# Running counts in PSUM beside an indirect scatter: one edit to a graph-network kernel's setup

## What is computed

```
edge_index = stack([src, dst])
h = relu(layernorm(x));  x = x + L0(h)   # messages x[dst] * filter(edge_weight), summed over src
h = relu(layernorm(x));  x = x + L1(h)   # two attention layers, softmax over the edges of one dst
h = relu(layernorm(x));  x = x + L2(h)   # edge MLP with edge_attr_64, mean over dst
h = relu(layernorm(x));  x = x + L3(h)   # 8-head attention over the edges of one dst
```

## Time and profile before

| | before |
|---|---|
| median of 3 runs | 7402.07 us |
| the profiled execution | 7404.54 us, span 7402.5 us |
| DVE busy over the span | 3299.0 us (45%) |
| POOL busy over the span | 5000.4 us (68%) |
| setup: next stage's first instruction | at 1304 us |
| L440, POOL's scatter | 782 DMAs, 791.2 us busy, 1012 ns each |
| L647, DVE's scans | 439 and 427 ns each |

### The profile page before, as it was taken

How to read it: one execution, slowest core, us unless ns; L and a number is a source line. 1 busy time by engine, 2 the same in 40 slices (tenths; PEclk the granted TensorE clock), 3 DMA queues, 4 the chain that set the end, 5 groups by cost and what they waited for, 6 DMA issues and landing times. The chain is left out here.

```text
span 7402.5 us, 89274 instructions
## 1 busy us (share of the span) xinstructions
PE 3331.8 (45%) x17325; PEld 2957.3 (40%) x17326; DVE 3299.0 (45%) x10231; ACT 1691.6 (23%) x4176; POOL 5000.4 (68%) x5176
## 2 busy tenths in 40 slices
PE   2200000444443864444434444445777775444443
PEld 1100000444443753444434444434777664344443
DVE  8777732333323663333344333335333336544445
ACT  2200000211111963222223222223222224000000
POOL 1677777677777726777755777764777770777775
PEclk9655555666666986555556555566666677666666
DMA  6122234444443624444434444433444440444443
GB/s 225 57 92 91 96 97 151 153 156 156 155 154 133 218 79 136 129 134 131 133 91 129 133 133 130 133 100 107 134 135 134 134 128 30 132 132 133 132 132 105
DMA packets 507505, 942.53 MB, mean 127 GB/s; under 512 B 204347, under 2 KB 240683, under 8 KB 507304
## 3 DMA queue, kind: packets, MB, share of 16 engines
q1 hardware_dynamic: 349288, 637.41, 25.9%
q0 software_dynamic: 158144, 304.31, 15.8%
HBM read 673.90 MB, written 270.84 MB: 128 GB/s over the span
## 5 line engine op out<-in xcount | busy, mean ns | idle before, releaser
L1371 POOL DMA_INDIRECT edge_buf<-node_table,ixr x1664 | 1571.6, 944 | 619.4 <-issue 507.9
L1371 POOL DMA_INDIRECT Y<-node_table,ixr x1664 | 1569.7, 943 | 521.1 <-issue 519.9
L1111 DVE TENSOR_TENSOR ACC<-ACC,bank 128x129 f32 (+2 forms) x3744 | 1092.9, 292 | 1102.2 <-PE bank L1098 469.2
L1279 POOL DMA_INDIRECT layer_messages<-edge_buf,ixr x832 | 809.3, 973 | 295.7 <-issue 263.0
L1538 PE MATMUL bank<-adc,turned_buf 128*128 x2496 | 340.3, 195 | 1476.1 <-issue 571.7
L440 POOL DMA_INDIRECT edge_records<-edge_buf x782 | 791.2, 1012 | 255.1 <-issue 246.2
L1538 PEld LDWEIGHTS bank<-adc,turned_buf 128*128 128x128 bf16 x2496 | 257.0, 103 | 1606.7 <-issue 1552.4
L1098 PE MATMUL bank<-edge_buf,Y 128*128 128x129 f32 (+2 forms) x3744 | 821.1, 406 | 142.7 <-ACT edge_buf L1524 96.5
L1098 PE MATMUL bank<-Y 128*128 128x129 f32 (+1 forms) x3328 | 763.1, 420 | 158.6 <-ACT Y L1524 88.7
L1098 PEld LDWEIGHTS bank<-edge_buf,Y 128*128 128x128 f32 x3744 | 764.0, 309 | 173.1 <-DVE ACC L1111 136.7
L1098 PEld LDWEIGHTS bank<-Y 128*128 128x128 f32 x3328 | 713.4, 323 | 181.5 <-issue 89.0
(11 more groups left out here) (279 smaller groups left out, 5319.1 us busy)
## 6 DMA issues: line engine op xcount, KB each, us to landing
Y<-onehots SPq DMA_DIRECT2D x416, 512.0 KB, 3.6
turned_buf<-onehots_turned SPq DMA_DIRECT2D x312, 256.0 KB, 3.8
edge_buf<-edge_records SPq DMA_DIRECT2D x208, 288.0 KB, 2.9
onehots<-Y SPq DMA_DIRECT2D x104, 512.0 KB, 2.7
layer_messages<-ACC SPq DMA_DIRECT2D x28, 1584.0 KB
XI<-layer_messages SPq DMA_DIRECT2D x78, 528.0 KB, 3.7
edge_records<-H SPq DMA_DIRECT2D x1, 29952.0 KB
onehots_turned<-turned_buf SPq DMA_DIRECT2D x104, 256.0 KB
```

Of the source, the lines that this page charges most:

```text
L1111: nc.vector.tensor_tensor(acc, acc, places.at(q, j, w), ALU.add).then_inc(added, 1)
L1279: pool.indirect_dma_start(msg_d, bass.IndirectOffsetOnAxis(ap=ixr[h][:, j:j + 1], axis=0), rows[h][:, j, 0:MW], None, bounds_check=SLOTS - ...
L1371: pool.indirect_dma_start(ring[q][:, j, 0:w], None, table, bass.IndirectOffsetOnAxis(ap=ixr[q][:, j:j + 1], axis=0)).then_inc(rows_in[q], 16)
```

## The change

For chunks 1 to 6 the tile `cum` of each h moves from SBUF to PSUM (bank 2 for h = 0, bank 3 for h = 1, 2 x 112 fp32 columns each). The second tensor of the scan, which the bypass does not use, becomes 112 columns of bank 1, set to zero once ahead of the loop. `eq`, `offs` and `slots` stay in SBUF. Chunk 0 stays as it was.

```diff
+            cums_psum = [bank[2 + h][:, 0:2 * CH].rearrange("p (q c) -> p q c", q=2) for h in range(2)]
+            unread = bank[1][:, 0:CH]
...
+                            running = cums if helped else cums_psum
+
                             def step(n, work):
                                 for h in range(2):
-                                    work(h, eqs[h], cums[h], bass.ds(i * 2 + h, 1))
+                                    work(h, eqs[h], running[h], bass.ds(i * 2 + h, 1))
...
                             def running_count(h, eq, cum, b):
                                 for q in range(2):
-                                    v.tensor_tensor_scan(cum[:, q, :], eq[:, q, :], eq[:, q, :], offs[0:EP, q, b],
-                                                         ALU.add, ALU.bypass).then_inc(count, 1)
+                                    v.tensor_tensor_scan(cum[:, q, :], eq[:, q, :], eq[:, q, :] if helped else unread,
+                                                         offs[0:EP, q, b], ALU.add, ALU.bypass).then_inc(count, 1)
...
                         slot_rows(0, st.then)
 
+                        st.then(v.memset(unread, 0.0))
                         with dve.Fori(1, CHUNKS) as c:
```

## The result

The kernel with the change takes 7372.8 us (median of seven runs, 7369.9 to 7375.9), the kernel before in the same comparison 7401.5 us (7399.5 to 7413.7). The ratio is 0.996, 95% interval 0.9949 to 0.9971: faster by 28.7 us. The first four experiments ran on a chip on which the kernel before takes 8976.4 us, the others on two chips on which it takes 7402.0 and 7401.1 us.

The account below looks back on a forecast made before the run. POOL's indirect DMAs were taken to bound the setup. The profiled 7404.5 us less 28.1 of delay is 7376.4; with the median of the runs 2.5 us under it, the forecast was 7374 us, range 7366 to 7392.

Parts of the forecast that it names:

- The path: Setup: POOL's 782 indirect DMAs set its pace from 250.5 us on; SyncE's padding ends last but moves with them.
- The term: POOL's scatter, L440: the whole delay of DMAs starting under scan, mask or addition goes, 28.1 us.
- The cause of the delay: L440's DMAs starting under L647, L655 or L658, with two SBUF tensor inputs, wait for the instruction's rest: 1.064 against 0.972 us.
- the prediction's own exception: One scatter DMA of 3.98 us at 1197.4 us starts under the relu L211; its 3.0 us stay, as the diff leaves L211 alone.
- the scans' case: Rival, chunks 1 to 6: scans, also reading `offs` from SBUF, go on delaying; 16.6 of 28.1 us stay, 7391 us; 5%.
- DVE at no price: DVE's rounds, chunks 1 to 6: ten instructions a round read or write PSUM at no added time.
- The cover: DVE's rounds beside the scatter: each may grow by 0.70 us before POOL waits; today's end is met again at 0.87 us.
- The formula: If DVE sets the pace at T a chunk, the last scatter starts at 250.5 + 6T and ends 144.9 us later.
- The parts: Shares of the 28.1 us by DMA starts in chunks 1 to 6: scans 16.6, masks 5.7.
- Mask: Rival, chunks 1 to 6: masks, whose SBUF tensor is the second input, go on delaying; 5.7 of 28.1 us stay, 7380 us; 5%.
- No effect: Rival, POOL's scatter: the delay comes from DVE's being busy with fp32 streams as such and stays whole; 7402 us; 5%.
- DVE as the bound: Rival, DVE's rounds: PSUM doubles the scan's streaming part, 1.27 us a round; the last DMA ends 59 us late, 7461 us; 6%.

Follow-up runs that it names:

- The first four experiments: Changed kernel with only the scan's second tensor, or only the counts, in PSUM; or with two more additions a round (one or two SBUF inputs): 8987.7, 8988.9, 9026.9, 9031.7 us.
- e7: Changed kernel with SyncE's last two padding writes issued behind its first load instead of its last: 7372.1 us, ratio 0.9958 to the kernel before.
- e5: Changed kernel with four more additions a round in chunks 1 to 6, each with one SBUF input: 7407.0 us, ratio 1.0005 to the kernel before.
- The scans alone: Changed kernel with the counts back in SBUF, only the scan's unused second tensor in PSUM: 7384.3 us, ratio 0.9977 to the kernel before.
- the rest alone: Changed kernel with the counts in PSUM but each scan reading `eq` twice, without the memset: 7384.9 us, ratio 0.9977 to the kernel before.
- e1: Changed kernel with the counts back in SBUF, only the scan's unused second tensor in PSUM: 8987.7 us against 8976.4, ratio 1.0011.

## Why the prediction was right

*The path.* POOL's pace was said to set the setup's end, with the padding moving along. The end of the scatter's last DMA went from 1288.2 to 1260.7 us, the padding's issue came 27.5 us earlier and the next stage too, at 1276.56 (forecast: DMA near 1260, stage near 1276). That SP's padding ends last was read rightly too; e7 shows 4.4 us for it.

*The term.* 28.1 us were forecast, the busy time fell by 791.2 - 763.5 = 27.7 us. That all of it would go rested on rows of later stages, in both orders of the operands; both orders hold in L659 and L662. One of those rows shows less than was read from it: the DMA at 3001.07 us starts 8 ns before the instruction of L1111 that it was put under. The trace as a whole bears the reading out, with 85 DMAs of L1371 that start under L1111 with over 0.2 us left and take 0.944 us (median), at most 0.947. The median moved by 28.7 us, 1 us more than the setup, which the runs' own spread covers.

*The cause of the delay.* Two SBUF tensors were named as what the three lines have in common. For these lines that was right, and the change needed no more. As a rule for all of DVE it was too narrow: the prediction's own exception, the relu L211, has one SBUF tensor, and `equal_to` (L643) delays as well. The argument from L643 against the scans' case (it has a tensor and a pointer in SBUF and its starts take 0.97) therefore proved nothing, since nearly all its starts came too late in it to be delayed. The conclusion held all the same: scans with one SBUF tensor and the pointer `offs` delay none of 172 starts. "The start waits for the rest" was right but for the last 0.13 to 0.20 us.

*DVE at no price.* Scans 439 to 442 ns, masks 393 to 400, additions 392 to 387: right to within 7 ns an instruction. The column update became cheaper (182 to 155 ns) and the two comparisons L647 too (619 to 599 ns together), for which the prediction had nothing; a round starts every 4.79 us instead of 4.88. Behind the cover it is worth nothing. The Trainium skill (page "VectorE: DVE Perf Modes", section "The TRN2 errata") has fixed costs of 58 cycles from SBUF and 120 from PSUM at 0.96 GHz, which is, as an estimate, 65 ns more an instruction. The additions of 128x224 show a difference of -5 ns, and here the measurement decides.

*The cover.* "It decides from 0.87 us a round": e5 added 0.86 to the round of the kernel before (5.74 against 4.88) and came out at 1.0005. The formula was 6 us short there, for the reason given above.

*The parts.* Here the prediction was wrong, and the forecast did not need them, because everything went. It shared the 28.1 us out as 16.6 for the scans and 11.5 for the rest. The scans alone gave 16.1 (791.2 - 775.1), the rest alone 18.4. What failed is the assumption that the places of POOL's starts in DVE's round stay as they are when a part of the delay goes.

*The rivals.* Mask and scans: both refuted by the table above. No effect and DVE as the bound: refuted on the chips of 7401 us. On the first chip DVE set the pace in the traces that were taken there, but through idle time at issue, not through the price of PSUM, which was the mechanism I had named; the change itself did not run there.

## What to carry to other kernels

Where GpSimd's indirect DMAs set the pace, look at each one's duration against what runs on VectorE at its start: if the longer ones begin under two-tensor instructions whose tensors both lie in SBUF, giving one of the two a place in PSUM takes the delay away; here it cost VectorE nothing. An operand that an operation doesn't use counts as one of the two. A `tensor_scalar` from SBUF to SBUF held DMAs up with its one tensor; a long one costs most, and can be moved to another engine, as the relu here. Before you call an instruction harmless, look at how early in it the DMAs start: one that is met only in its last 0.13 us shows no delay whatever it is. Don't add up shares of such a delay from where the starts fall now; take one away and the others fall elsewhere.

## What the runs showed that I had not expected

On one chip VectorE's rounds beside the scatter were mostly 22 to 25 us apart instead of 4.8 (e1), idle at issue before L647 and before scans and additions (270.1, 181.4 and 97.7 us), while the instructions themselves took as long as elsewhere. With POOL idle, from 410 to 485 us, the rounds there were 4.77 us again. The windows of those 75 us and of the next 111, in which the scatter runs again, show DVE's count:

```profile
410.00:485.00 75.00, 0.00 (x0) 0.00 (x0) 56.79 (x192) 0.61 (x4) 0.00 (x0) 0.50 0.03 12
485.00:596.00 111.00, 0.00 (x0) 0.00 (x0) 31.52 (x97) 1.77 (x10) 82.42 (x84) 0.50 0.25 78
```

(Columns: stretch, us, then busy time and count of PE, weight load, DVE, ACT, POOL; granted clock, share of DMA, GB/s.) 192 instructions in 75 us, then 97 in 111. What VectorE's issue waits for there was not found: no run took the scatter away on that chip.

The other surprise is how well two loops fall into step: with rounds of 5.13 us, 135 of 144 were of the same length to within 5 ns. A DMA that is 25 ns ahead after each round is held for just those 25 ns, and so a delay that could have been 0.2 us stayed at a tenth of that.
